# MoE feed-forward: the projection down in two halves behind the second and third expert product, in a PSUM bank each; the residual in halves, the statistics behind the fourth product

## The reference, cut to what matters

```python
x = x + _L0_ffn_ref(_layernorm(x, axis=-1), ...)

def _L0_ffn_ref(hidden_states, gate_w, correction_bias, Wg, Wu, Wd, Wg_s, Wu_s, Wd_s):
    ...                                  # cw: weight of each expert for each token
    g = jnp.einsum('nh,ehi->eni', x, Wg)
    u = jnp.einsum('nh,ehi->eni', x, Wu)
    y = jnp.einsum('eni,eih->enh', jax.nn.silu(g) * u, Wd)
    routed = jnp.einsum('enh,ne->nh', y, cw)
    out = routed + _mlp(x, Wg_s, Wu_s, Wd_s)
```

## Time and profile before

| what | value |
|---|---|
| median of 3 runs (range) | 919.32 us (918.39 to 922.0) |
| profiled execution, its own time | 919.77 us |
| its span, first to last instruction | 918.0 us |
| TensorE matmuls busy | 636.6 us (69%) |
| VectorE busy | 640.3 us (70%) |
| ScalarE busy | 381.0 us (42%) |
| GpSimd busy | 286.7 us (31%) |
| mean granted clock of TensorE | 0.844 |

### The profile page before, as it was taken

One profiled execution on the slowest core, in us unless ns is written; L12 is line 12 of the kernel. 1 busy time (PEld: TensorE's weight loads), 2 busy tenths in 40 slices (PEclk: granted clock), 3 DMA queues, 4 the chain that ended last, 5 costly groups with the idle time before them and its releaser, 6 DMA issues.

```text
span 918.0 us, 22815 instructions
## 1 busy us (share of the span) xinstructions
PE 636.6 (69%) x9634; PEld 452.8 (49%) x9634; DVE 640.3 (70%) x1232; ACT 381.0 (42%) x905; POOL 286.7 (31%) x276
## 2 busy tenths in 40 slices
PE   3899999899999999999997789894200000000686
PEld 1688887566666666666566555474000000000674
DVE  6367876376766676666746562467999999998767
ACT  2556666532333333332223221237655454444124
POOL 6456555100000000000020001202578788787310
PEclk9989999999999999999999599997655555555567
DMA  5100000000000000000000013000000000000001
GB/s 188 21 6 14 15 15 13 3 3 2 11 5 2 4 12 2 2 2 2 2 3 1 1 34 60 1 1 1 0 0 0 0 0 0 1 0 0 2 1 46
DMA packets 8069, 11.05 MB, mean 12 GB/s; under 512 B 1296, under 2 KB 5648, under 8 KB 7840
## 3 DMA queue, kind: packets, MB, share of 16 engines
q1 hardware_dynamic: 7968, 9.60, 4.0%
HBM read 6.41 MB, written 1.08 MB: 8 GB/s over the span
## 4 chain that ended last, share of the span: by engine, by line
PE 55%; DVE 22%; issue 13%; POOL 5%; ACT 3%; DMA 1%; SPq 0%; DVEq 0%; POOLq 0%; ACTq 0%
PE PS L587 9%; PE PS L562 7%; PE PS L460 5%; PE PS L356 4%; PE PS L344 4%; PE PS L330 4%; PE PS L717 3%; PE PS L579 2%; PE PS L467 2%; PE PS L730 2%; PE PS L294 2%; DVE arena L1267 2%; DVE arena L1275 2%; PE PS L731 2%; POOL arena L1154 1%
## 5 line engine op out<-in xcount | busy, mean ns | idle before, releaser
L643 DVE TENSOR_TENSOR arena<-PS,C 128x512 f32<-128x512 f32 x160 | 105.5, 686 | 97.0 <-PE PS L562 97.0
L934 PE MATMUL PS<-arena 64*64 64x8 f32 x112 | 8.4, 255 | 196.3 <-DVE arena L1319 192.3
L1051 ACT ACTIVATE arena<-arena 128x128 f32<-128x128 f32 x256 | 81.8, 390 | 94.3 <-DVE arena L1275 94.3
L934 PEld LDWEIGHTS PS<-arena 64*64 64x64 f32 x112 | 7.1, 212 | 199.0 <-DVE arena L1287 193.9
L587 PEld LDWEIGHTS PS<-arena 128*64 128x64 f32 x2560 | 83.6, 138 | 40.0 <-issue 38.1
L1549 POOL TENSOR_TENSOR arena<-arena 128x512 f32<-128x512 f32 x4 | 5.0, 1274 | 305.0 <-PE PS L587 305.0
L562 PE MATMUL PS<-arena 64*64 64x512 f32 x640 | 87.1, 614 | 3.4 <-ACT arena L516 2.0
L1137 POOL TENSOR_TENSOR arena<-arena 128x1024 f32<-128x1024 f32 x32 | 75.2, 2350 | 41.6 <-DVE arena L1275 41.6
L587 PE MATMUL PS<-arena 128*64 128x18 f32 x2560 | 87.2, 211 | 0.0
L418 POOL TENSOR_TENSOR arena<-arena 128x512 f32<-128x512 f32 x64 | 66.6, 1041 | 54.5 <-DVE arena L401 50.7
L491 ACT ACTIVATE arena<-PS 128x512 f32<-128x512 f32 (+1 forms) x48 | 23.5, 524 | 129.9 <-PE PS L462 71.8
(11 more groups left out here) (252 smaller groups left out, 1470.6 us busy)
## 6 DMA issues: line engine op xcount, KB each, us to landing
W<-wpack SPq DMA_DIRECT2D x1, 2532.5 KB, 10.9
arena<-arena SPq DMA_DIRECT2D x128, 16.0 KB
arena<-carry_in SPq DMA_DIRECT2D x4, 512.0 KB, 7.8
X<-x SPq DMA_DIRECT2D x4, 256.0 KB, 3.7
out<-X SPq DMA_DIRECT2D x4, 256.0 KB, 2.3
C<-cpack SPq DMA_DIRECT2D x1, 529.0 KB, 6.5
wk<-wkT SPq DMA_DIRECT2D x1, 64.0 KB, 10.9
wv<-wvT SPq DMA_DIRECT2D x1, 64.0 KB, 11.4
```

The costliest lines, as they stand in the source:

```text
L643: e.tensor_tensor(AT[n % 4].rearrange("p (h t) -> p h t", h=8), PS[:, n % 2, :].rearrange("p (h t) -> p h t", h=8), tri.to_broadcast([P, 8 ...
L1051: e.activation(Ra[:, cols], Rs[(t - 1) % 4][:, cols], ACT.Copy, scale=alp[:, t, h:h + 1]).then_inc(l_Ra, 1)
```

## The change

The projection `down(tb, half)` does two of the four tiles at a time. The first half stands behind the pair of `q` = 1 as the whole did, the second behind the pair of `q` = 2. The first half of every block goes to bank 6, the second to bank 7. The residual follows in halves of 256 columns: the first behind the product of `q` = 2, the second behind that of `q` = 3, and the statistics move there with it. The first half's residual has a semaphore of its own, `x_half`, so that `x_upd` still counts whole blocks; `f_out` counts halves.

```diff
-            def down(tb):
-                e.wait_ge(f_a2, 5 * (tb + 1))
-                if tb >= 2:
-                    e.wait_ge(x_upd, 4 + tb - 1)
-                if tb == 1:
-                    e.wait_ge(f_cs, 2)
-                for i in range(4):
+            def down(tb, half):
+                if half == 0:
+                    e.wait_ge(f_a2, 5 * (tb + 1))
+                    if tb >= 1:
+                        e.wait_ge(x_half, tb)
+                else:
+                    e.wait_ge(x_upd, 4 + tb)
+                    if tb == 0:
+                        e.wait_ge(f_cs, 2)
+                for i in (2 * half, 2 * half + 1):
                     for q in range(5):
...
-                        m = e.matmul(PS[:, 6 + tb % 2, i * P:(i + 1) * P], act[tb % 2][0:k, q, i * P:(i + 1) * P], wd,
+                        m = e.matmul(PS[:, 6 + half, i * P:(i + 1) * P], act[tb % 2][0:k, q, i * P:(i + 1) * P], wd,
...
-                if q == 1 and tb > 0:
-                    down(tb - 1)
-            down(NQ - 1)
+                if q in (1, 2) and tb > 0:
+                    down(tb - 1, q - 1)
+            down(NQ - 1, 0)
+            down(NQ - 1, 1)
...
-            def residual(tb):
-                e.wait_ge(f_out, tb + 1)
-                xs = X[:, 4 * tb:4 * tb + 4, :]
-                e.tensor_tensor(xs, PS[:, 6 + tb % 2, :].rearrange("p (j d) -> p j d", j=4), xs, ALU.add).then_inc(x_upd, 1)
+            def residual(tb, half):
+                e.wait_ge(f_out, 2 * tb + half + 1)
+                xs = X[:, 4 * tb + 2 * half:4 * tb + 2 * half + 2, :]
+                m = e.tensor_tensor(xs, PS[:, 6 + half, 2 * P * half:2 * P * (half + 1)].rearrange("p (j d) -> p j d", j=2),
+                                    xs, ALU.add)
+                m.then_inc(x_half if half == 0 else x_upd, 1)
...
                 if q == 0 and tb >= 2:
-                    e.wait_ge(f_out, tb - 1)
+                    e.wait_ge(f_out, 2 * (tb - 1))
...
                 if q == 2 and tb > 0:
-                    residual(tb - 1)
+                    residual(tb - 1, 0)
+                if q == 3 and tb > 0:
+                    residual(tb - 1, 1)
                     ln_moments(e, 2, tb - 1)
```

More of the change, by code:

```diff
@@ L206, in program @@
         x_upd = sem("x_upd")
+        x_half = sem("x_half")
         xbo = sem("xbo")
@@ L855, in moe_dve @@
                 ln_scale(e, 2, q)
-            residual(NQ - 1)
+            residual(NQ - 1, 0)
+            residual(NQ - 1, 1)
             ln_moments(e, 2, NQ - 1)
```

## The result

The changed kernel takes 926.53 us in the median of 20 runs (919.46 to 929.68), the kernel before 920.16 (915.63 to 924.12). The ratio is 1.0055 with a 95% interval of 1.0034 to 1.0076, that is 5.1 us more (3.1 to 7.0). The means lie 5.1 us apart too, the medians 6.4. The change makes the kernel slower by a little over 0.5%. I had said 921.5, between 918.8 and 924.2, with 0.08 for slower by more than 0.5%. Of the 5.0 us between 921.5 and 926.53, 0.8 is the kernel before, whose median was 919.32 over three runs and is 920.16 here.

The account below looks back on a forecast made before the run. The prediction took TensorE to bound the MoE loop. Waits of +0.6 us and a lost clock of +1.6 us made +2.2, forecasting 921.5 us against the median 919.32, range 918.8 to 924.2.

Parts of the forecast that it names:

- Waits: TensorE's waits in the MoE loop: -0.16 and +0.73, together about +0.6 us, up to +1.6 with bounds.
- removed waits: TensorE before steps 14 and 19 (n = 5 tb + q): two waits of 1.20 us go, hidden by the half projection.
- the bare chain before step 15: Only step 14 lies between the pairs of steps 13 and 15, so 15 starts 4.90 us after 13; wait some 1.2.
- The three stretches: TensorE: block before the second projection 0, second to third projection -0.16, third to last +0.73 us.
- step 11's: Block before the second projection: the moved statistics delay step 11 by at most 0.52 us; taken as 0.
- That the clock is lost: TensorE idle 3.41 us before the last projection loses its full clock; 0.61 for one spell, 0.08 for low through the tail.
- What the loss costs: Work after the last wait: 3.4 us at the lower level loses 1.6 us, bounds 0 and 3.3 for two spells.
- the row of 636 to 642: Earlier trace after 4.71 us idle: grants 0.81 and 0.62, 3.4 us at the lower level, used as the spell's length.
- slice 23 of the page: Just ahead of the MoE loop: mean grant 0.5 to 0.6 over 22.95 us, so a lost clock may stay longer.
- the rival that the clock stays low: Half rate from the last projection through the fourth transposes adds some 10 us, about 930; chance 0.08.
- That the split pays: Rival: the two waits of 1.20 us go and nothing comes back, 916.9 us; chance 0.11.
- the four idle pieces of 4.48 us: TensorE before steps 14, 15, 19 and the last projection: 1.20, 0.69, 1.20, 1.39 us, all the change could win there.

Follow-up runs that it names:

- the one with fillers behind the wait: Changed kernel with 24 filler matmuls after the wait for the last product, ahead of the last projection; one profiled execution, 925.63 us.
- the run with the statistics alone: Kernel before with only the statistics moved behind the fourth product, projection and residual whole; 1.0002 of the kernel before, median 920.13 us.
- the run with the idle piece alone: Kernel before with 11 spare statistics on VectorE ahead of the product of step 19; 1.0057 of the kernel before, median 926.01 us.
- the run with fillers: Changed kernel with 24 filler matmuls on TensorE in the wait ahead of the last projection; 0.9996 of the kernel before, median 918.05 us.

## Why the prediction was wrong, by its own steps

**Waits: right.** The removed waits and the bare chain before step 15 came as worked out (1.05 for 1.2; the pair of 15 starts 4.90 after that of 13, 572.85 to 577.75). The timeline of VectorE in the changed kernel has the half residual that the trace before did not have, and the two late products:

```profile
576.91 0.69 DVE L844 TENSOR_TENSOR arena<-arena,PS 128x512 f32<-128x512 f32 x1 [3.70 <-POOL arena L823]
577.52 0.42 DVE L833 TENSOR_TENSOR X<-PS,X 128x256 f32<-128x256 f32 x1
577.97 0.87 DVE L271 BATCH_NORM_STATS2 st<-X 128x6 f32<-128x128 f32 x4
...
579.23 0.67 DVE L851 TENSOR_TENSOR arena<-arena,PS 64x512 f32<-64x512 f32 x1
...
593.90 0.69 DVE L844 TENSOR_TENSOR arena<-arena,PS 128x512 f32<-128x512 f32 x1 [4.07 <-POOL arena L823]
...
596.22 0.67 DVE L851 TENSOR_TENSOR arena<-arena,PS 64x512 f32<-64x512 f32 x1
```

From product to product it is 2.32 us both times, as estimated from the earlier trace rows. The three stretches measured +0.12 (step 11's, taken as 0), -0.28 (565.23 to 581.85 is 16.62; I had 16.74) and +0.99 (581.85 to 596.95 is 15.10; I had 14.84). Together they are +0.83, where I had +0.6 and a range of 0.4 to 1.6. The last stretch is 0.26 longer than worked out: product 18 starts 4.43 after its pair instead of 4.06, 0.37 more, and the pieces ahead of that pair are 0.10 shorter. The chain of work has 0.41 us there that it calls issue, in which VectorE waited for nothing that the profile shows; the cause is open.

**That the clock is lost: right.** I placed 3.41 us of idle between the 2.58 and 4.71 of the earlier trace rows and gave 0.61 + 0.08 to its loss. It was 3.63.

**What the loss costs: wrong, and this made the error.** I sized the spell by the row of 636 to 642, 3.4 us, and priced it at 1.6 us with an upper bound of two spells. It lasted 10.3 us and cost 4.62, and the projection took 9.98 us where I had named 7 to 8. With 0.83 for the waits that makes 5.45, where the sum had +2.2. In that row TensorE ran other matmuls (line 914), and I took its length for one that holds for any work. The runs show that it does not: 10.2 to 10.3 us in all four profiles that lost the clock ahead of the projection, 3.4 in the one with fillers behind the wait. I had seen the other kind myself, slice 23 of the page, and used it only for the rival that the clock stays low. Against that rival I wrote that the projection is dense. It was dense, 3.00 us busy of 3.00, and the clock came back only 1.5 us behind its end. That rival's own condition, over 8 us at the lower level, is what happened, at its small end (5.45 us in all, not 10). So its price belonged into the range, with more of the chance than 0.08. The range's upper end is the sum of the upper bounds (919.32 + 1.6 + 3.3); its lower end, 918.8, lies 0.9 under the sum of the lower ones.

The Trainium skill, "TensorE: Matmul & The Clock Gate", section "Why this matters for your kernels", whose rule on idle gaps I weighed, has the clock fall back behind a long one. Ahead of the last projection 1.57 and 1.92 us kept the clock, and 2.64, 3.52, 3.61, 3.62 and 3.63 lost it; the gap that the section names is longer than 2.64 and than the 2.58 of the earlier trace rows, so its figure does not fit these two, and there the measurement decides. The same section has matmuls that run on without a break get past the half rate. Under the projection that took 10.2 us at the lower level, and what it depends on the section does not say.

**The rivals.** That the split pays is refuted for this placing: the four idle pieces of 4.48 us became three of 5.03 (1.05, 0.35 and 3.63). With the statistics one product later 1.5 us of waits do go.

## What to carry to other kernels

When a wait is removed on TensorE, look for what runs late behind the next one. Here a wait of 1.2 us would have hidden the late product, as the run with the statistics alone shows; with it gone the idle time gathered in one piece, and the 3.6 us in one piece lost the clock, which four pieces of 4.5 us together had kept. Price a lost clock by a row in which TensorE did the same kind of work as it will do then, and let the upper bound cover the longer stretches that the trace shows elsewhere (here slice 23 of the page). Put fillers into an idle piece that can't be closed: 24 of them gave the 0.5% back here.

## What the runs showed that I had not expected

The projection's matmuls (128x128, float32) bring the clock back late. In four profiles (idle 2.64, 3.52, 3.61 and 3.63 us) the projection took 10.28, 10.45, 10.10 and 9.98 us, though in none of them did TensorE pause in it, and by their windows the clock was low for 10.2 to 10.3 us each time. In three of them it came back 0.7 to 1.5 us behind the projection's end. In the run with the idle piece alone it had fallen at 596.0, in the wait, and came back at 606.3, 0.8 us ahead of the end, so there the projection brought it back without other work:

```profile
596.00:599.00 3.00, 2.40 (x10) 2.18 (x10) 2.93 (x12) 0.00 (x0) 0.00 (x0) 0.50 0.00 0
599.00:602.00 3.00, 3.00 (x12) 2.38 (x11) 1.22 (x6) 0.00 (x0) 0.00 (x0) 0.50 0.00 0
602.00:605.00 3.00, 3.00 (x12) 2.50 (x12) 0.00 (x0) 0.00 (x0) 0.00 (x0) 0.50 0.00 0
605.00:608.00 3.00, 3.00 (x19) 2.70 (x20) 0.88 (x2) 0.33 (x1) 0.15 (x1) 0.79 0.00 0
```

At full clock the same records keep the clock and take 6.08. The fillers differ from them in type and in columns; which of the two makes the difference, if either does, was not taken apart.

The length of one idle piece is not the whole of it either. In the profile of the run with fillers the clock fell at 462 us, ahead of the change, though the longest idle piece in the 15 us before was 1.01 us; the changed kernel's profile has the same piece there and kept its clock. What decides between the two is not shown.
